# Linear attention without a value projection, loops written out in a line, and a LayerNorm that writes its kept tokens directly

## The reference

```
def _layernorm(x): m, v = mean(x), var(x); return (x - m) / sqrt(v + 1e-5)

# linear attention: 16 heads of 64, x is [4, 1024, 128]
q = x @ wq + bq;  k = x @ wk + bk;  v = x @ wv + bv
qm, km = elu(q) + 1, elu(k) + 1
kv = einsum('nshd,nshm->nhmd', km, v)
z  = 1 / (einsum('nlhd,nhd->nlh', qm, sum(km, axis=1)) + 1e-6)
y  = einsum('nlhd,nhmd,nlh->nlhm', qm, kv, z)
out = einsum('nlhm,hmf->nlf', y, wo) + bo
```

## Time and profile before

| | us |
|---|---|
| median of 3 runs | 5035.45 (5034.88 to 5036.51) |
| profiled execution, its own time | 5037.02 |
| its span | 5035.2 |
| granted TensorE clock, mean | 0.95 of full |
| instructions | 75510 |
| linear attention without its LayerNorm, in the trace | 1268.7 to 1665.6 |
| experts0, first | 1018.5 to 1244.2 |
| rope_project, first | 47.6 to 113.2 |

### The profile page before, as it was taken

The page is one execution under the profiler, slowest core; times in us unless marked ns, Lnnn a source line. Parts: engine busy times, 40 slices in busy tenths (PEclk is TensorE's granted clock), DMA queues, the critical chain, the costliest instruction groups (busy, mean ns, idle before and its releaser), DMA issues. The chain is left out here.

```text
span 5035.2 us, 75510 instructions
## 1 busy us (share of the span) xinstructions
PE 4533.3 (90%) x25425; PEld 2134.6 (42%) x25425; DVE 3608.2 (72%) x8320; ACT 2332.0 (46%) x3145; POOL 812.9 (16%) x655
## 2 busy tenths in 40 slices
PE   4899999788999679999978989969999999998998
PEld 2222222443454312222244467744444444444776
DVE  6799999466666779999945677765656556556776
ACT  3477777422444337777742244433333333334443
POOL 3000000001000300000000000014444444443000
PEclk9799999799999879999988989979999999998999
DMA  3111111200000211111120010000000000001000
GB/s 94 37 41 43 41 42 41 94 0 30 1 0 0 59 49 39 45 38 45 39 78 23 0 38 1 1 21 2 2 2 2 2 2 2 2 2 39 1 0 17
DMA packets 233732, 127.60 MB, mean 25 GB/s; under 512 B 162152, under 2 KB 197916, under 8 KB 233308
## 3 DMA queue, kind: packets, MB, share of 16 engines
q1 hardware_dynamic: 225276, 106.04, 7.9%
q0 software_dynamic: 6432, 17.57, 1.4%
q10 hardware_dynamic: 1728, 0.28, 0.0%
HBM read 85.94 MB, written 36.70 MB: 24 GB/s over the span
## 5 line engine op out<-in xcount | busy, mean ns | idle before, releaser
L645 DVE TENSOR_REDUCE ra_mh<-PS 128x1 f32<-128x512 f32 x2144 | 1341.6, 681 | 153.3 <-PE PS L523 144.3
L600 ACT ACTIVATE ra_p<-PS 128x1024 f32<-128x1024 f32 x1040 | 1011.8, 1021 | 482.9 <-PE PS L530 474.6
L523 PE MATMUL PS<-ra_k,ra_q 96*128 96x512 bf16 x2144 | 749.8, 392 | 3.5 <-DVE ra_mh L645 3.2
L539 PE MATMUL PS<-ra_p,ra_va 128*32 128x512 f32 x4192 | 569.8, 608 | 70.5 <-ACT ra_va L593 70.3
L530 PE MATMUL PS<-ra_q,ra_k 99*128 99x512 bf16 x2080 | 622.5, 380 | 1.7
L1812 ACT ACTIVATE ca_p<-PS 128x1024 f32<-128x1024 f32 (+3 forms) x384 | 310.8, 809 | 589.2 <-PE PS L1742 384.6
L1881 DVE TENSOR_REDUCE ca_mh<-PS 128x1 f32<-128x512 f32 (+3 forms) x768 | 388.1, 551 | 153.1 <-PE PS L1702 123.8
L1441 ACT ACTIVATE f_hh<-PS,f_b 128x512 f32<-128x512 f32 x448 | 302.8, 687 | 390.4 <-PE PS L1397 390.1
L523 PEld LDWEIGHTS PS<-ra_k,ra_q 96*128 96x128 bf16 x2144 | 202.0, 97 | 660.9 <-DVE ra_mh L645 499.5
L1407 PEld LDWEIGHTS PS<-f_w,f_hh 128*128 128x128 f32 x3584 | 432.9, 192 | 99.5 <-issue 65.1
L1847 POOL TENSOR_TENSOR ca_s<-ca_s,ca_p 128x1024 f32<-128x1024 f32 (+3 forms) x256 | 414.0, 1617 | 234.8 <-ACT ca_p L1812 229.5
(11 more groups left out here) (242 smaller groups left out, 5481.2 us busy)
## 6 DMA issues: line engine op xcount, KB each, us to landing
ra_k<-qk_parts SPq DMA_DIRECT2D x136, 144.0 KB
ra_q<-qk_parts SPq DMA_DIRECT2D x408, 48.0 KB
o_heads<-ra_ot POOLq DMA_DIRECT2D x134, 128.0 KB, 2.9
ao_ot<-o_heads SPq DMA_DIRECT2D x16, 1024.0 KB, 6.4
qk_parts<-rp_parts SPq DMA_DIRECT2D x96, 128.0 KB, 2.3
ra_vc<-v_heads SPq DMA_DIRECT2D x34, 128.0 KB, 5.8
v_heads<-rp_vs SPq DMA_DIRECT2D x64, 64.0 KB, 1.9
ra_q<-ra_mp SPq DMA_DIRECT2D x198, 4.0 KB, 1.7
```

What stands on the lines that cost most here:

```text
L523: pe.matmul(PS[:, 5 + place % 3, :], Q[0:KMAX, u, j, t * P:(t + 1) * P], K[0:KMAX, u, j, h * BT:(h + 1) * BT], start=True, stop=True).then ...
L539: mm = pe.matmul(PS[VW * j:VW * (j + 1), 4, :], VA[:, ub, step % KT, j, :], PR[:, s % 2, j, :], start=(s % KT == 0) if start is None else ...
L600: act.activation(PR[:, s % 2, PH * pair:PH * (pair + 1), :], PS[:, PH * pair:PH * (pair + 1), :], ACT.Exp, scale=float(DH) ** -0.5).then_i ...
L645: dve.tensor_reduce(mh[:, pair, c // HALVES, c % HALVES:c % HALVES + 1], PS[:, bank, :], AX.X, ALU.max).then_inc(s_max, 1)
```

## The change

1. **Loops.** Every `Fori` becomes a Python `for` over the same range, in LayerNorm, rope_project, attention_output, experts0, linear_attention and ffn1. Waits and addresses become constants; the order of operations on each engine stays.
2. **LayerNorm.** DVE writes its result straight into XN; PE transposes from XN. `ln_xn`, ACT's copy to XN, ACT's drain and DVE's wait for `copied` go; PE waits for the copy two blocks back.
3. **Linear attention.** A head's values and output weights are joined: M = Wv Wo per head, and the bias part BW, are prepared in the first batch (`prepare`, after gathers 1, 3, 5 and 6, with four ACT copies). Values are not projected. Keys are projected straight from XNT. The gather is XN^T times km (512 columns, banks 4 and 5), its result A is copied by ACT and multiplied by M. POOL sums km over the tiles (`kms`), PE reduces it with a tile of ones (`key_sums`), DVE builds G = BW * ks + A M. The query ring has four banks, its first two tiles are issued in the key phase. The spread of the inverses is four matmuls of 32 rows into four banks at once. The output has qm stationary and G moving, so that it comes out in token layout: no copy, no turn. The output bias is added to all of X once, by POOL. The next batch's first key tile is projected ahead of the spread, its second after the outputs.

```diff
 class LayerNorm (vector, tensor, scalar)
-        with dve.Fori(0, NBLK // 2) as it:
+        for it in range(NBLK // 2):
...
-                dve.wait_ge(self.copied, 2 * n)
                 for j in range(TPB):
-                    dve.tensor_scalar(xn[:, u, j, :], X[:, TPB * n + j, :], mv[:, u, j, 0:1],
+                    dve.tensor_scalar(self.XN[:, TPB * n + j, :], X[:, TPB * n + j, :], mv[:, u, j, 0:1],
...
-                pe.wait_ge(self.copied, 2 * n)
+                if n >= 2:
+                    pe.wait_ge(self.copied, n - 1)
...
-        act.drain().then_inc(self.copied, 2)
-                act.wait_ge(self.normed, TPB * n + TPB)
-                act.activation(self.XN[:, bass.ds(TPB * n, TPB), :], self.xn[:, u, :, :], ACT.Copy).then_inc(self.copied, 1)

 linear_attention, PE
+                def prepare(i):
+                    if i:
+                        pe.wait_ge(s_pc, i)
...
+                            if i == 0:
+                                mm = pe.transpose(PS[:, bank, cols], wv[:, p * P:(p + 1) * P], IDN[:, :])
+                            elif i == 3:
+                                mm = pe.matmul(PS[:, bank, cols], G[:, p, :], wo[:, p, :], start=True, stop=True)
+                            else:
+                                mm = pe.matmul(PS[:, bank, cols], wvT[rows_, p, :], wo[rows_, p, :], start=True, stop=True)
+                def project_k(b, t):
+                    i = KT * b + t
+                    if t >= 3:
+                        pe.wait_ge(s_rd, i - 1)
+                    elif b:
+                        pe.wait_ge(s_sc if t else s_g, QS * b if t else NP * b)
+                    for c in range(CB):
+                        mm = pe.matmul(PS[:, keys(t) + c, :], XNT[:, i * P:(i + 1) * P], wk[:, c * BT:(c + 1) * BT],
+                                       start=True, stop=True)
+                def gather(b, t):
+                    pe.wait_ge(s_km, i + 1)
+                    for c in range(CB):
+                        mm = pe.matmul(PS[:, 4 + c, :], XN[:, i, :], km[:, i % RB, c * BT:(c + 1) * BT], start=(t == 0),
+                                       stop=(t == KT - 1))
+                def key_sums(b):
+                    pe.wait_ge(s_sum, (KT - 1) * (b + 1))
...
+                    for p in range(NP):
+                        mm = pe.matmul(PS[:, 6, HD * p:HD * (p + 1)], kms[:, p * P:(p + 1) * P], ones[:, :], start=True, stop=True)
+                def multiply(b):
+                    pe.wait_ge(s_ate, b + 1)
+                    for p in range(NP):
+                        for h in range(2):
+                            mm = pe.matmul(PS[HD * h:HD * (h + 1), 4 + p // PB, p % PB * P:(p % PB + 1) * P], AT[:, p, h, :],
+                                           M[:, h, p, :], start=True, stop=True, skip_group_check=True)
+                def spread(b, c, half):
+                    pe.wait_ge(s_z, CHUNKS * (n + 1))
+                    pe.wait_ge(s_eq, 2 * QS * (b + 1))
+                    if c or half:
+                        pe.wait_ge(s_sc, NP * n + PB * half)
+                    for r in range(PB):
+                        part = slice(32 * r, 32 * (r + 1))
+                        mm = pe.matmul(PS[:, r, :], sel[part, PB * half + r, :], z[part, c, :], start=True, stop=True)
+                def output(b, c, pairs):
+                    for p in pairs:
+                        pe.wait_ge(s_sc, NP * n + p + 1)
...
+                        for j in range(TPB):
+                            mm = pe.matmul(PS[:, 6 + c, j * D:(j + 1) * D], qm[:, c, p, j * P:(j + 1) * P], G[:, p, :],
+                                           start=(p == 0 and j == 0), stop=(p == NP - 1), skip_group_check=True)
...
+                    for k in range(QS):
+                        if k >= 2:
+                            project(b, k)
+                        if k + 1 == SUMS:
+                            key_sums(b)
+                        if k + 1 == MULTIPLY:
+                            multiply(b)
+                        if k + 1 == DENOM:
+                            denominators(b, 0)
+                    if b + 1 < BATCH:
+                        project_k(b + 1, 0)
+                    spread(b, 0, 0)
+                    denominators(b, 1)
+                    output(b, 0, (0, 1, 2))
+                    spread(b, 0, 1)
+                    output(b, 0, (3, 4, 5))
+                    spread(b, 1, 0)
+                    output(b, 0, (6, 7))
+                    output(b, 1, (0, 1, 2))
+                    spread(b, 1, 1)
+                    output(b, 1, tuple(range(3, NP)))
+                    if b + 1 < BATCH:
+                        project_k(b + 1, 1)

 linear_attention, POOL
+                pool.tensor_tensor(X[:, 0:NT, :], X[:, 0:NT, :], bc(bo[:, :], [[0, NT], [1, D]]), ALU.add).then_inc(s_xb, 1)
...
+                        pool.wait_ge(s_km, i + 1)
...
+                        pool.tensor_tensor(kms[:, :], old, km[:, i % RB, :], ALU.add).then_inc(s_sum, 1)

 linear_attention, DVE (behind query tile MULTIPLY)
+                            for q in range(NP):
+                                dve.scalar_tensor_tensor(G[:, q, :], BW[:, q, :], ks[:, q:q + 1],
+                                                         PS[:, 4 + q // PB, q % PB * D:(q % PB + 1) * D],
+                                                         ALU.mult, ALU.add).then_inc(s_g, 1)
```

More of the change, by code:

```diff
@@ L160 @@
 class LayerNorm:
[L164 removed]
+    COPIES = NBLK
     def __init__(self, g, sb, sem):
@@ L215, in tensor @@
     def tensor(self, pe):
-        with pe.Fori(0, NBLK // 2) as it:
+        for it in range(NBLK // 2):
             for u in range(2):
@@ L313, in _ @@
                 pe.wait_ge(s_w, 6)
-                with pe.Fori(0, BATCH) as b:
+                for b in range(BATCH):
                     for u in range(2):
@@ L358, in _ @@
                 dve.tensor_copy(wv[:, 2:4, :, 1], wv[:, 0:2, :, 0]).then_inc(s_w, 1)
-                with dve.Fori(0, BATCH) as b:
+                for b in range(BATCH):
                     for u in range(2):
@@ L730, in _ @@
             def _(sp):
-                with sp.Fori(0, BATCH) as b:
+                for b in range(BATCH):
                     for u in range(2):
@@ L815, in _ @@
             def _(pool):
-                with pool.Fori(0, BATCH) as b:
+                for b in range(BATCH):
                     for u in range(2):
@@ L944, in _ @@
             def _(pool):
-                with pool.Fori(0, NBLK) as n:
+                for n in range(NBLK):
                     pool.wait_ge(s_ms, n + 1)
@@ L1314, in ffn1 @@
+                    for p in range(PB):
+                        scale(b, 0, p)
+                    denominators(b, 1)
+                    for p in range(PB, NP):
+                        invert(b, 1, p - PB)
+                        scale(b, 0, p)
+                    for p in range(PB):
+                        scale(b, 1, p)
+                    add(b, 0)
+                    for p in range(PB, NP):
+                        scale(b, 1, p)
+                    add(b, 1)
 def ffn1(nc, a, g):
@@ L1431, in _ @@
                 act.wait_ge(s_h0, 80)
-                with act.Fori(0, NBLK // 2) as it:
+                for it in range(NBLK // 2):
                     for u in range(2):
```

401 lines of the change are left out of this document (197 added, 204 removed).

## The result

The median fell from 5035.16 to 4926.6 us (4925.9 to 4927.3); the ratio is 0.9783 with a 95% interval of 0.9771 to 0.9795. The forecast was 4916 with a range of 4893 to 4950. The profiled execution took 4927.3 (span 4925.5), against 5037.0 before: 109.7 us less, where the sum said 119.

A forecast was written before the change was run, and what follows sets the result against it. PE's own work was taken to bound linear attention. Terms of -91, -17, -4, -2 and -5 made -119 us against the profiled 5037.0, so 4918, or 4916 as median; range 4893 to 4950.

The forecast's parts named there:

- its own bounds: Linear attention: forecast change of -91 us, with bounds of -95 to -86.
- the forecast's own signs of being wrong: Period over 78 us; DVE's 1024-wide operations over 1.7 us beside POOL; linear attention's clock under 0.95; experts0 keeping 225 us.
- the walk's times: Linear attention: new order followed on all engines through one batch, giving 73.7 us, 8.5 of it idle, against 98.3.
- Sum 65: Linear attention: PE's work per batch after the change, added up from prices per matmul, 65 us.
- I take +4, nearer the unharmed 280: Linear attention: POOL working beside DVE costs +4 us, chosen between bounds 0 and +9.
- the bound of 2.2: Linear attention: upper bound per batch for POOL's cost beside DVE, +9 us in all.
- The 280 row: Earlier trace: a two-input 16 x 128 operation beside POOL's additions takes 280 ns, a cast 1645; read as disagreeing with the skill.
- The rival of a lower clock: Linear attention: PE held at its low clock, +260 us if all its work ran at 1.2 GHz, 5176; chance 0.03.
- -22.1 for -17: experts0, sixteen blocks in two stages: loops in a line save 17 us, bounds 0 and -29.
- -8.2 for -5: LayerNorm, eight blocks in six stages: half of DVE's wait for POOL goes, -5 us (0 to -10).
- -3.5 for -4: rope_project, two stages: less address arithmetic for SP's stores saves 2 us each, -4 (0 to -8).
- -3.8 for -2: attention_output: loops in a line save 2 us (0 to -3).

The follow-up runs named there:

- e4_lines_only: The kernel before with every loop written out in a line and nothing else changed; 4998.5 us, ratio 0.9925.
- e1: The kernel after with POOL's seven additions of km per batch only 8 columns wide instead of 1024, every wait kept; 4923.45 us.
- e8: The kernel after with one more POOL addition of two 512-wide halves of km ahead of each of the seven sums; 4967.7 us.
- after_again: The kernel after, unchanged, measured again in the same rounds as two later variants; 4927.4 us.
- e6_order: The kernel after with key sums issued behind the fourth query tile, multiply behind the seventh and denominators behind the tenth; 4923.9 us.

## Why the prediction was right, and which term was not

*The sum and the signs.* The time is right: 4926.6 lies in the range, and in the forecast's own range of 4900 to 4935. But two errors met there, one of +20.6 in linear attention, whose -70.4 lies outside its own bounds, and one of -11 in everything else. That they partly cancelled is luck. And two of the forecast's own signs of being wrong came true: the period is over 78 (78.81), and beside POOL a 1024-wide operation of DVE took longer than 1.7 (2.86). The other two did not: the stage's granted clock was 0.98, and experts0 took 215.9.

*What bounds the stage.* Right. Columns taken from PE were time: 72 us by e4_lines_only against after. That DVE and ACT would trail at four places was right as well: by the walk's times PE waits before the denominators, the first spread, the third spread and the first gather, for 1.95, 1.55, 2.1 and 2.15; they measured 1.87, 1.52, 1.74 and 1.84. The idle time as a whole, 8.9 for 8.5, agrees less well than it looks: 1.72 of it (0.22, 0.68 and 0.82) are waits for km and for POOL's sum of it, which the walk did not have.

*The walk's step that failed: PE's prices.* "Sum 65" should have been 69.9. Outputs were priced by columns (0.86) from rows with 512 moving columns; with G's 128 they need 0.93 (4.66 for five), and 15.3 for all sixteen where 13.8 was forecast: 1.5 per batch. Four 32-row tiles take 1.07, not 0.86: 0.85 per batch. The sixteen query tiles took 14.6 for 13.8, as they stand in small groups. Key sums were an estimate of 1.2 and took 1.84, multiply 1.90 for 1.7, denominators 1.85 for 1.7, twice. The last 0.7 are gathers and key projections that stand beside a wait (1.82 for the gather of 1341.78, where 1.72 was forecast). Together that makes the 4.9 per batch, but for rounding. The Trainium skill ("TensorE: Matmul & The Clock Gate", section "Why this matters for your kernels") gives 3.07 times for four such tiles; the estimate from it, 1.12 per spread, is nearer to the measured 1.07 than my 0.86.

*POOL beside DVE.* "I take +4, nearer the unharmed 280" was the wrong row. That operation has two inputs in SBUF, but the combination behaves like the cast: e1 gives 2.39 us per batch, above the bound of 2.2, and 7.2 in the three batches that gained, not far under the bound of 9; POOL's own time is in it. The Trainium skill ("GPSIMD Engine Reference", section "Key points") says that GpSimd contends with DVE instructions of two SBUF inputs; the 1.64 us lost at 1362.62 and e8 agree with it. The 280 row does not speak against it, as the start times in the trace of before show, which the forecast had not set side by side. DVE's cast and two-input operation, and POOL's additions around them (two in the row, each 2.35 or less):

```profile
3457.71 1.69 DVE L1898 CAST ca_mp<-ca_nr 16x128 bf16<-16x128 f32 x1
3459.43 0.28 DVE L1899 TENSOR_TENSOR ca_mp<-ca_nr,ca_mp 16x128 bf16<-16x128 f32 x1
...
3456.97 4.42 POOL L1847 TENSOR_TENSOR ca_s<-ca_s,ca_p 128x1024 f32<-128x1024 f32 x2 [0.57 <-ACT ca_p L1812]
```

The cast of 3457.71 ends at 3459.40, just after POOL's first addition, begun at 3456.97, has had its 2.35 us. The two-input operation starts at 3459.43, in the gap between the two additions. So the cast did the waiting, and the operation behind it met no addition at its start.

*The clock.* The rival of a lower clock was right in kind at a fraction of its size. The stage's share beyond four periods is 12.3 us (327.5 - 4 x 78.81) where it was 4.6; of the 7.7 the preparation explains 3.7 (PE's four pieces take 0.88, 1.09, 1.10 and 1.79 in the first batch, and PE's start is no longer 1.2 behind the xs copy), where 3.3 was forecast. The windows at 0.85 and 0.84 (20 us each) lose 3.0 and 3.2, against 2.1 in the 30 us at 0.93 before: 4.1 more. In the trace of the kernel after the clock fell within the stage, once its start was over, in the last batch alone; in that of after_again it fell in the first two as well.

So linear attention: 4 x 5.1 = 20.4 by the period and about 4 at the ends, less the 4 that the forecast had set aside for POOL.

*experts0.* -22.1 for -17, and part of that is luck. The pitch was right (0.385 for the forecast 0.39), and so was the edge: the two waits fell from 1.27 and 0.96 to 0.61 and 0.37, 1.25 of 2.2 where 1.1 was forecast. But the forecast gave both to each of sixteen blocks. PE's waits in the first stage, before and after (total, times, longest), show that a block's edge has one or the other:

```profile
PE PS L919 <- DVE e_acc L996: 14.4, 5, 10.6
PE PS L911 <- DVE e_y L1001: 3.8, 3, 1.3
...
PE PS L914 <- DVE e_acc L991: 11.5, 5, 10.0
PE PS L906 <- DVE e_y L996: 1.8, 3, 0.6
```

Three edges of one kind and four of the other gave 4.3 us, not 8.8. The window lost 9.8 all the same, 5.1 of them idle and 4.7 in PE's busy time. Of the latter 1.5 stand behind the one long wait, where the eight records of L919 took 6.74 (1048.36) and those of L914 5.21 (1041.43), both partly at the lower clock (0.70 granted from 1035 to 1058 before, 0.78 from 1029 to 1052 after). Why the other 3.2 fell the rows do not tell.

*LayerNorm.* -8.2 for -5: the whole wait for POOL (0.2) went, not half, but it stood in every second block. The mean step fell from 2.455 to 2.32, which makes 6.5 us in 48 blocks; the rest stands at the stages' starts and ends. *rope_project* -3.5 for -4; *attention_output* -3.8 for -2. ffn1 and causal moved by about 2 us in all, as said.

## What to carry to other kernels

Price matmuls by rows of the same shape: the same columns in 128-wide pieces, or in small groups between waits, cost 5 to 10% more, and in a stage bound by PE that is the forecast's error. Before work goes to POOL beside a busy DVE, line up the start times of both engines: what counted here is how much of a DVE operation with two SBUF inputs fell under a POOL operation, and how long PE then waited for POOL's own result. Once an engine's work has shrunk, the order of what stands behind each wait is worth a look of its own: here moving a few operations, and two additions to DVE, gave 19 us more.

## What was not expected of the hardware

- DVE's combination of two SBUF tiles and POOL's addition hold each other up nearly completely, both ways (1.64 us lost for 1.77 of overlap; 3.34 instead of 2.36 for POOL), while DVE's addition with a PSUM input kept 1.23 us.
- The same wait of 1.74 us is followed in one batch by full speed (five outputs in 4.73) and in another by 5.80. e6_order's executions lie up to 7 us apart, more than some of the edits are worth; the fastest had a mean granted clock of 0.951, the other three, of which no trace is kept, 0.949. So differences of 3 us between kernels need the period of an undisturbed batch beside the median, counted between two like points that no slow stretch precedes. What sets the clock off was not tried.
- Hardware loops cost 38 us of 5035, in stages whose bounding engine looked 87% busy, and nothing in linear attention, whose PE was never late behind them.
